# A state-space and gated-recurrence kernel: the order of the loads between two stages, and one semaphore for each slot

## The reference, cut to what matters

```
r: (8, 2048, 512)                                  # batch, time, channel
y1 = causal_conv(layernorm(r), K) + D * layernorm(r)   # K from 64 complex poles
x1 = r + layernorm(gelu(y1))
xt = layernorm(x1)                                 # the recurrence's input
for step in range(8):                              # r's first axis is the scan's; c is (2048, 512)
    f = sigmoid(xt[step] @ wf.T + c @ uf.T + bf)
    i = sigmoid(xt[step] @ wi.T + c @ ui.T + bi)
    g = tanh(xt[step] @ wc.T + c @ uc.T + bc)
    c = f * c + i * g
h  = tanh(xt @ wo.T + c_final @ uo.T + bo)
out = x1 + layernorm(h)
```

## Time and profile before

| | |
|---|---|
| median of 3 runs | 2644.72 us (2644.36 to 2645.83) |
| the profiled execution: its time | 2645.57 us |
| its span in the profile | 2643.9 us |
| mean granted TensorE clock | 0.983 of 2.4 GHz |
| PE busy | 2527.1 us, 96% |
| DVE, ACT, POOL busy | 1837.5, 1626.2, 1128.8 us (70, 62, 43%) |
| DMA moved | 542.52 MB, 205 GB/s on average |

### The profile page before, as it was taken

The page is one execution under the profiler, slowest core; times in us unless marked ns, Lnnn a source line. Parts: engine busy times, 40 slices in busy tenths (PEclk is TensorE's granted clock), DMA queues, the critical chain, the costliest instruction groups (busy, mean ns, idle before and its releaser), DMA issues.

```text
span 2643.9 us, 57576 instructions
## 1 busy us (share of the span) xinstructions
PE 2527.1 (96%) x22659; PEld 2202.8 (83%) x22659; DVE 1837.5 (70%) x3409; ACT 1626.2 (62%) x3013; POOL 1128.8 (43%) x1433
## 2 busy tenths in 40 slices
PE   5499999997899999999999999999999999999998
PEld 4278888886788888888888888888888888888887
DVE  7855556558887677776777887777677774467667
ACT  8756667566655555555556665555555554379777
POOL 7778686725332223222234332322222320068667
PEclk9799999998999999999999999999999999999999
DMA  8769797889674455445665755544456432489998
GB/s 352 291 230 315 265 314 271 269 296 341 181 196 116 129 141 164 124 116 127 146 164 149 195 161 142 168 123 116 126 140 163 127 85 49 157 333 352 367 360 347
DMA packets 507551, 542.52 MB, mean 205 GB/s; under 512 B 273936, under 2 KB 412944, under 8 KB 488720
## 3 DMA queue, kind: packets, MB, share of 16 engines
q1 hardware_dynamic: 507280, 538.85, 65.2%
HBM read 292.88 MB, written 180.88 MB: 179 GB/s over the span
## 4 chain that ended last, share of the span: by engine, by line
PE 84%; POOL 4%; DVE 4%; ACT 3%; DMA 3%; issue 2%; SPq 1%; DVEq 0%; POOLq 0%; ACTq 0%
PE bank L2162 31%; PE bank L2172 29%; PE bank L2218 8%; PE bank L2051 4%; PE bank L2001 3%; PE bank L2037 3%; PE bank L2059 2%; PE bank L2013 2%; PE bank L2193 2%; DVE big L1843 1%; PE bank L2021 1%; POOL big L891 1%; ACT big L1354 1%; POOL big L995 1%; DMA x1d<-big 1%
## 5 line engine op out<-in xcount | busy, mean ns | idle before, releaser
L2162 PE MATMUL bank<-big 128*128 128x256 f16 x8064 | 1081.0, 274 | 19.7 <-ACT big L1400 8.6
L2172 PE MATMUL bank<-big 128*128 128x256 f16 x7056 | 962.7, 273 | 0.0
L2162 PEld LDWEIGHTS bank<-big 128*128 128x128 f16 x8064 | 789.7, 98 | 118.6 <-ACT big L1400 9.9
L2172 PEld LDWEIGHTS bank<-big 128*128 128x128 f16 x7056 | 689.7, 98 | 80.5
L1036 POOL TENSOR_SCALAR big<-big 128x1 f32<-128x1 f32 x253 | 108.2, 427 | 1086.9 <-DVE big L1690 807.7
L1900 DVE TENSOR_TENSOR big<-bank,big 128x512 f32<-128x512 f32 x256 | 174.9, 683 | 198.2 <-PE bank L2172 194.6
L2218 PE MATMUL bank<-big 128*128 128x256 f16 x2688 | 295.5, 273 | 4.4 <-ACT bank L1334 4.0
L1310 ACT ACTIVATE big<-big 128x512 f32<-128x512 f32 x384 | 289.5, 803 | 14.1 <-DVE big L1900 14.1
L2218 PEld LDWEIGHTS bank<-big 128*128 128x128 f16 x2688 | 261.8, 98 | 37.8 <-ACT bank L1334 5.0
L1886 DVE TENSOR_TENSOR big<-bank,big 128x512 f32<-128x512 f32 x256 | 176.2, 688 | 141.6 <-PE bank L2172 119.8
L1242 ACT ACTIVATE big<-big 128x512 f32<-128x512 f32 x256 | 206.0, 808 | 101.4 <-POOL big L1038 98.0
(11 more groups left out here) (234 smaller groups left out, 3719.5 us busy)
## 6 DMA issues: line engine op xcount, KB each, us to landing
xtd<-big SPq DMA_DIRECT2D x60, 1024.0 KB, 6.6
big<-xr SPq DMA_DIRECT2D x16, 2048.0 KB, 9.1
big<-xg SPq DMA_DIRECT2D x64, 512.0 KB, 8.0
big<-kpad SPq DMA_DIRECT2D x32, 1024.0 KB, 12.1
yd<-big SPq DMA_DIRECT2D x16, 2048.0 KB, 16.7
big<-x SPq DMA_DIRECT2D x128, 256.0 KB, 3.3
x1d<-big SPq DMA_DIRECT2D x128, 256.0 KB, 3.2
big<-x1d SPq DMA_DIRECT2D x64, 512.0 KB, 8.8
```

The lines of the kernel that those rows point to most:

```text
L2162: ins = e.matmul(o, WX[2 * g + lw][:, q, kt, 128 * a:128 * a + 128], slot[u % 2][:, part, lx, k0 + kt, :], start=(first and kt == 0 and (l ...
L2172: ins = e.matmul(o, WC[2 * g + lw][:, q, kt, 128 * a:128 * a + 128], cc[unit(u)[1] % 2][:, qc, lx, kt, :], start=False, stop=end, skip_gro ...
```

## The change

It is in SP's program alone. In the loop over groups, at i = 16, a block is added that issues, after the wait for `cv` at 480 (the last group but one is convolved): the sums `fbs`, the four chunks of r of unit 0, `WX[4]`, `WX[5]`, `WC[0]`, then `load_y(0)` and `store_y(14)`. These were issued behind the loop, in the order `load_y(0)`, two chunks, `fbs`, two chunks, `store_y(14)`, and the three weight parts only after `load_y(1)` and the chunks of unit 1. Behind the loop, `load_y(1)` now stands after two of unit 0's four `store_x1` instead of after all, `WC[1]` stands ahead of the chunks of unit 1, and these behind it. Each transfer is still issued once.

`store_xt(v)` now raises `xs0` for even and `xs1` for odd units, in both halves, `turn` waits for all of the slot's earlier stores by that count, and the two waits between `store_xt(0)` and `store_xt(1)` are gone.

`load_y` and `load_x1` are moved up in the text, without a change in them. The rest of the diff:

```diff
@@ sync_program, loop over i, before weights(-1)
+                if i == NG:
+                    w.wait_ge(s["cv"], G * (NG - 1))
+                    w.wait_ge(s["accs"], 16 * 3)
+                    e.dma_start(fbs, accd.rearrange("g p h -> p g h")).then_inc(s["accs"], 16)
+                    for c in CHUNKS:
+                        load_x1(0, c)
+                    w.wait_ge(s["wx"], 16 * 4)
+                    load_WX(4)
+                    load_WX(5)
+                    load_WC(0)
+                    load_y(0)
+                    store_y(NG - 2)
                 weights(-1)
@@ turn
-                    w.wait_ge(s[f"xs{k // 2}"], 16 * (v - 1))
+                    w.wait_ge(s[f"xs{v % 2}"], 32 * (v // 2))
@@ store_xt, both transfers
-                    e.dma_start(xtd[v][:, 2 * r:2 * r + 2]..., slot[v % 2][:, 2 * r:2 * r + 2]...).then_inc(s[f"xs{r}"], 16)
+                    e.dma_start(xtd[v][:, 2 * r:2 * r + 2]..., slot[v % 2][:, 2 * r:2 * r + 2]...).then_inc(s[f"xs{v % 2}"], 16)
@@ prepare, between store_xt(0), load_WC(5) and store_xt(1)
-                    w.wait_ge(s["xs0"], 16)
-                    w.wait_ge(s["xs1"], 16)
@@ behind the loop over i
-            w.wait_ge(s["cv"], G * (NG - 1))
-            load_y(0)
-            for c in CHUNKS[:2]:
-                load_x1(0, c)
-            w.wait_ge(s["accs"], 16 * 3)
-            e.dma_start(fbs, accd.rearrange("g p h -> p g h")).then_inc(s["accs"], 16)
-            for c in CHUNKS[2:]:
-                load_x1(0, c)
-            store_y(NG - 2)
             store_y(NG - 1)
             w.wait_ge(s["cv"], G * NG)
-            for r in range(4):
+            for r in range(2):
                 store_x1(0, r)
             load_y(1)
-            for c in CHUNKS:
-                load_x1(1, c)
-            w.wait_ge(s["wx"], 16 * 4)
-            load_WX(4)
-            load_WX(5)
+            for r in range(2, 4):
+                store_x1(0, r)
             w.wait_ge(s["w_lo"], low_base(8))
             w.wait_ge(s["wd"], stored(7))
             w.wait_ge(s["fb"], 12)
-            load_WC(0)
             load_WC(1)
+            for c in CHUNKS:
+                load_x1(1, c)
```

More of the change, by code:

```diff
@@ L601, in load_WC, with load_y, load_x1 @@
                 e.dma_start(WC[n].rearrange("p q k f -> p q (k f)"), wg[2 * g + 1][:, l]).then_inc(s["wc"], 16)
+            def load_y(v):
+                b, j = unit(v)
+                src = yd[:, :, b, 4 * j:4 * j + 4, :].rearrange("g t k h -> t g k h")
+                if v == 0:
+                    w.wait_ge(s["y0"], 16 * 7)
+                    w.wait_ge(s["y1"], 16 * 7)
+                    e.dma_start(yt[:, 0:NG - 2], src[:, 0:NG - 2]).then_inc(s["yl"], 16)
+                    return
+                w.wait_ge(s["y0"], 16 * 8)
+                w.wait_ge(s["y1"], 16 * 8)
+                if v == 1:
+                    w.wait_ge(s["yc"], 2)
+                elif v == 2:
+                    w.wait_ge(s["x1"], 4)
+                    w.wait_ge(s["yl"], 32)
+                else:
+                    w.wait_ge(s["ss"], 8 * v)
+                    w.wait_ge(s["xh"], 8 * v - 2)
+                    w.wait_ge(s["xlo"], 8 * v - 2)
+                e.dma_start(rows_y(v), src).then_inc(s["yl"], 16)
+            def load_x1(v, c):
+                b, j = unit(v)
+                if v == 1:
+                    w.wait_ge(s["x2"], 4)
+                    w.wait_ge(s["xl%d" % c], 32)
+                elif v:
+                    w.wait_ge(s["xh"], 8 * (v - 1) + 4 * (c % 2) + 4)
+                    w.wait_ge(s["xlo"], 8 * (v - 1) + 4 * (c % 2) + 4)
+                e.dma_start(xb[c], x[b, 512 * j + 128 * c:512 * j + 128 * c + 128, :]).then_inc(s[f"xl{c}"], 16)
             e.dma_start(sm, small).then_inc(s["sm"], 16)
@@ L670, in sync_program @@
                     weights(j)
[L672 to L703, removed]
             def store_x1(v, r):
@@ L724, in store_xt @@
                     w.wait_ge(s[f"xq{2 * r + 1}"], 32 * v)
-                    e.dma_start(xtd[v][:, 2 * r:2 * r + 2].rearrange("p q l k t -> p (q l k t)"), slot[v % 2][:, 2 * r:2 * r + 2].rearrange("p q l k t -> p (q l k t)")).then_inc(s[f"xs{r}"], 16)
+                    e.dma_start(xtd[v][:, 2 * r:2 * r + 2].rearrange("p q l k t -> p (q l k t)"), slot[v % 2][:, 2 * r:2 * r + 2].rearrange("p q l k t -> p (q l k t)")).then_inc(s[f"xs{v % 2}"], 16)
             def prepare(v):
@@ L832, in sync_program @@
                 w.wait_ge(s[f"xq{c}"], 32 * (NU - 1))
-            w.wait_ge(s["xs0"], 16 * (NU - 2))
-            w.wait_ge(s["xs1"], 16 * (NU - 2))
+            for r in range(2):
+                w.wait_ge(s[f"xs{r}"], 16 * (NU - 2))
             e.dma_start(Uo, wd).then_inc(s["wu"], 16)
```

## The result

The change makes the kernel slower by 0.39%: 2655.38 us median of 5 runs (2653.58 to 2656.54) against 2644.72 (2644.21 to 2645.83, 5 runs on the same chip), ratio 1.0039 with a 95% interval of 1.0027 to 1.005. I had put 2652.3. The profiled execution took 2656.54 with a span of 2654.7, so the span grew by 10.8 us where my sum says 7.6. Executions of one kernel lie up to 5 us apart (2641.55 to 2646.39 in 33 of the kernel before), so the difference of two single profiles is known less well than that of two medians.

What follows compares the result with a forecast made beforehand. TensorE's matmul count was taken to bound the kernel, with PE gaps before 684 carried to the end. The terms +9.5, -1.1 and -0.8 gave +7.6 us on the 2644.72 median: 2652.3 us, range 2641 to 2656.

Steps and rivals of the forecast that it cites:

- main case: Whole kernel: +9.5, -1.1 and -0.8 sum to +7.6 us, 2652.3; own range 2649.5 to 2656; chance 0.60.
- D: Last y store: SP, blocked, issues it late, y1 passes 624.3 and adds up to 3 us; 2655.5; chance 0.05.
- load_y(0) goes from first to ninth: Start of unit 0: y0 behind eight other issues lands at 602.9, so VectorE's chain shifts by +10.7 us.
- lower bound of +4.0: y0's landing: if nothing ahead delayed it, it would land at 596.1, which is +4.0 us.
- rival A: y0's landing: transfers share engines evenly, y0 lands near 596.1, y1 bounds VectorE; +3.0 us, 2647.7; chance 0.12.
- The weight wait goes, ScalarE's copy limits: Unit 0 on PE: of the 1.95 us weight-part wait, ScalarE's copy lets 1.2 be gained; unit 0 ends 9.5 late.
- load_y(1) is hidden: Start of unit 1: y1 lands near 619.8, VectorE is free at 624.3; hidden with 4.5 us to spare.
- Relief in the transposes' gap: The 7.89 us PE gap at 640.9: SP reaches the next transpose sooner, -1.1 us, bounds 0 and -2.
- Semaphore by slot: Waits before store_xt(1): the full DMA queue, not SP's wait, holds the x1 stores; -0.8 us, bounds 0 and -5.4.
- Rival B: Unit 2's x1 stores: they land 5.5 us earlier and PE gaps close, -5.4; total +3.0, 2647.7; chance 0.13.
- Rival C: PE from 648.8 to 696: removing SP's wait returns gaps and clock, 14.1 us; total -5.7, 2639.0; chance 0.12.

Runs made afterwards that it cites:

- the order alone: The changed kernel with the old semaphores and the two waits put back, so only the new order of the loads: 2653.76 us, ratio 1.0035.
- the slots alone: The kernel before with only the semaphores by slot and without the two waits, loads in the old order: 2645.81 us, ratio 1.0005.
- x1 first: The slots alone, with store_xt(1) moved behind the first three store_x1 of unit 2: 2643.79 us, ratio 0.9995.
- the parts back: The changed kernel with load_y(0) behind the sums and x chunks, and the three weight parts back behind the loop: 2648.74 us, ratio 1.0016.
- y0 first: The changed kernel with load_y(0) first in the new block again: 2651.82 us, ratio 1.0028.
- y0 after x: The changed kernel with load_y(0) behind the sums and x chunks but ahead of the three weight parts: 2653.65 us, ratio 1.0037.
- the parts late: x1 first, with the weight parts WC3, WC4 and WC5 also moved behind store_xt(1): 2642.6 us, ratio 0.9995.
- all orders: The parts late, with WX4 and WX5 ahead of unit 1's last two chunks and two transposes ahead of unit 2's first chunks: 2643.69 us, ratio 0.9997.

## Why the prediction was right, and where its sizes were off

The time was higher than 2652.3 by 3.1, inside the main case's own range. That it lies inside is in part luck: the upper end of 2656 was there for D, which did not happen. With the bounds of steps 4 and 5 alone the range would have ended at 2654.2. (D's own time should read 2655.3 by its sum.) By its steps:

1. *load_y(0) goes from first to ninth*: right, and the largest term. y0's wait follows the bytes ahead of it in every kernel run, so the lower bound of +4.0 and **rival A** (y0 overtakes) are refuted. The size was +11.9 instead of +10.7. The formula from the Trainium skill's page "DMA: Bandwidth & Descriptors", section "Anatomy of one DMA", gave 600.3; the trace has 604.1, so it does not agree (the page fits it to one DMA of the software path), and the rows were nearer with 602.9. The landings say which term was too small. The sums land at 590.3, as put (590.4). The last of the four chunks lands at 594.1 where I had 592.8, so the chunks take 3.8 us instead of 2.4. The three parts follow at 596.3, 598.5 and 600.85, 6.75 instead of 6.45, and y0 takes 3.3 instead of 3.6. So the term of the sum that was mis-sized is the chunks', priced at the 418 GB/s of another stage. Why their 1.05 MB took 3.8 us, while the queue's share was 1.05 from 588.3 to 590.3 and 1.06 from there to 594.5, is not shown. The order alone waited 20.33 us for y0, 0.6 less, so half of the 1.2 is within what two traces differ by.

2. *The weight wait goes, ScalarE's copy limits*: right. Unit 0 took 651.51 - 624.01 = 27.50 us on PE instead of 640.88 - 612.11 = 28.77, 1.3 less where I had 1.2.

3. *load_y(1) is hidden*: right, with 4.7 us to spare where I had 4.5. It was closer to a bound than one term at nothing suggests: with y0 put first again, y1 is the bound and the kernel still 0.28% slower than before. The start of unit 1 that rival A gave for this case was 619.8; it is 619.91.

4. *Relief in the transposes' gap*: right, 0.9 instead of 1.1. The two transposes that took SP 4.53 us to issue before take 2.61 in the kernel after (the row at 648.65). The other kernels bear it out: where such a pair took SP 4.5 to 4.7 us (before, the slots alone, x1 first, the parts back) the gap was 7.7 to 8.2, and where it took 2.6 to 2.7 (after, the order alone, y0 first, y0 after x, the parts late) it was 6.5 to 7.0. (With all orders four transposes stand together there.)

5. *Semaphore by slot*: the reason was right (the queue, not SP's wait, holds the x1 stores), but -0.8 had the wrong sign. The gaps before and after sum to the same 8.12, GpSimd's wait grew, and the slots alone measure +0.05%, not separable from nothing. **Rival B** (paid in full, -5.4) is refuted by the slots alone. Taking GpSimd's wait away altogether left 7.4 us of gaps of 8.1, so its price of 5.4 was wrong as well: the gaps have other owners behind that one. **Rival C** needed 8.4 us returned. The gaps returned nothing, and the clock took another 0.9.

The excess of the span, 10.8 - 7.6 = 3.2: y0 1.2, unit 0 and the gap 0.1, step 5 0.8, and the lower clock of unit 1's stage 0.9, with 0.2 behind 731. The last two are within what one profile differs from another: the order alone has the same stage at clock 0.94 and 2.8 us shorter, with idle time 0.3 less. The slots can't be told from nothing either. So of the 3 us only y0's 0.6 to 1.2 can be laid to the change with some ground; the rest may be the spread of single profiles.

**Rival D** (later still, by y1 passing VectorE) did not happen in the kernel after, though the two y stores held SP for 11.10 us, from 589.39 to 600.5: 4.7 us of spare were left.

What stays open: what owns the 8 us of gaps in unit 1's stage. The runs show that they do not follow GpSimd's first wait, and no kernel run here closes them. One trace points to VectorE's addition of the last chunk and the transposes behind it; a kernel that moves that addition would test it.

## What to carry to other kernels

In a queue that is full and serves in order, moving a load forward moves another back by the time of its bytes (6.5 us for three parts here). Look for the load whose reader already waits, and put nothing ahead of it that is read 20 us later. And a wait on the issuing engine cost nothing that could be measured here while the transfers ahead of it still filled the queue: compare landing times, not issue times. Before pricing a gap by the one wait that ends last in front of it, ask what is ready just behind that wait; here one order removed it and two more shortened it, and most of the idle time stayed.

## What the runs showed of the hardware

- An earlier issue into a full queue came back nearly one for one as a longer time to landing: 4.0 us sooner by the trace's clock (5.0 counted from the stores before), 4.3 us longer to land.
- In a full queue SP itself is held in an issue. The first of the two y stores took SP 9.67 us to issue in the kernel after, from 589.39, and 0.33 us at 590.11 in the kernel before.
- The granted clock of one and the same stage of 517 matmuls was between 0.89 and 0.94 in the rows shown, with 61.5 to 64.4 us of busy time. That spread of 2.9 us is more than the 0.8 that step 5 put on the slots.
- All compute engines stood still from 601 to 604 with a granted clock of 0.50 (of the two levels, 1.2 GHz). The chain from VectorE's copy to the first product starts in that state, and it took 17.2 us in both kernels. Before it started at a mean of 0.75 (595 to 598) and went on at 0.50, so that the earlier standstill cost it nothing that shows.
